# A decoder layer on one core: attention's step order, bias and clears moved, and the next phase's first rows loaded ahead of the barrier

## What is computed

```python
# x: 4 batches x 512 tokens x 512 channels
x = layernorm(x + attention(x))   # 16 heads of 32 channels, causal, softmax, output projection with bias
x = layernorm(x + chosen(x))      # one of 4 SwiGLU experts per token, chosen by the token id
x = layernorm(x + routed(x))      # top 2 of 8 SwiGLU experts (F = 352) plus a shared one (1408)
```

## Time and profile before

| | |
|---|---|
| median of 3 runs | 1285.53 us (1281.93, 1285.53, 1288.90) |
| the profiled execution | 1281.12 us |
| its span, first to last instruction | 1279.4 us |
| attention phase | from 0 to 459.4 us |
| chosen phase | 459.4 to about 599 us |
| routed phase | from there to the end |
| PE busy over the span | 1183.3 us, 92% |
| DVE, ACT, POOL busy | 691.8, 455.7, 238.2 us |

### The profile page before, as it was taken

The page is one execution under the profiler, slowest core; times in us unless marked ns, Lnnn a source line. Parts: engine busy times, 40 slices in busy tenths (PEclk is TensorE's granted clock), DMA queues, the critical chain, the costliest instruction groups (busy, mean ns, idle before and its releaser), DMA issues.

```text
span 1279.4 us, 20171 instructions
## 1 busy us (share of the span) xinstructions
PE 1183.3 (92%) x6404; PEld 938.2 (73%) x6404; DVE 691.8 (54%) x1469; ACT 455.7 (36%) x698; POOL 238.2 (19%) x358
## 2 busy tenths in 40 slices
PE   7788999999999769995999999999999999899996
PEld 5555566566576558884678888899999998678885
DVE  5664556656657546664547744444344432676754
ACT  3244334433435222221433334244444443333331
POOL 2021312412513410002300441000000000433200
PEclk8989999999999879997899999999999999999998
DMA  7355663532523322223523566344444531656440
GB/s 241 84 168 163 222 187 106 151 93 51 141 64 89 108 82 83 83 83 94 170 74 99 177 223 211 92 150 138 150 152 146 186 106 42 205 178 199 142 140 33
DMA packets 129276, 169.72 MB, mean 133 GB/s; under 512 B 17552, under 2 KB 70800, under 8 KB 129168
## 3 DMA queue, kind: packets, MB, share of 16 engines
q1 hardware_dynamic: 115360, 136.64, 34.7%
q0 software_dynamic: 8496, 28.32, 6.6%
q10 hardware_dynamic: 5312, 3.42, 1.1%
HBM read 95.98 MB, written 47.19 MB: 112 GB/s over the span
## 4 chain that ended last, share of the span: by engine, by line
PE 52%; DVE 4%; POOL 2%; issue 2%; DMA 2%; ACT 1%; SPq 0%; ACTq 0%; DVEq 0%; POOLq 0%
PE routed_ps L808 17%; PE routed_ps L1361 16%; PE chosen_psG L808 4%; PE chosen_psY L808 4%; PE routed_ps L1380 2%; PE routed_ps L1381 2%; PE routed_ps L1382 2%; POOL routed_rows_io L1299 2%; PE routed_ps L1402 1%; DVE routed_held L1704 1%; PE routed_ps L1425 1%; PE chosen_psX L889 1%; DMA routed_wdraw<-in_L_ffn_Wd_dram 1%; PE chosen_psH L908 1%; PE routed_ps L1326 1%
## 5 line engine op out<-in xcount | busy, mean ns | idle before, releaser
L459 PE MATMUL psT<-store 128*128 128x512 f32 x576 | 159.9, 412 | 5.1 <-DVE store L673 3.2
L742 DVE CUSTOM_DVE_ANT_0 psS<-psS,attn_mask 128x512 f32<-128x512 f32 (+3 forms) x256 | 120.6, 514 | 54.6 <-PE psS L525 54.5
L629 ACT ACTIVATE acc<-psE 128x512 f32<-128x512 f32 x160 | 92.9, 598 | 147.5 <-PE psE L546 143.5
L1361 PE MATMUL routed_ps<-routed_later,routed_held 128*128 128x512 f32 x528 | 124.7, 392 | 5.9 <-issue 2.9
L1361 PE MATMUL routed_ps<-routed_first,routed_held 128*128 128x512 f32 x528 | 127.6, 395 | 1.4 <-DVE routed_first L1800 1.4
L459 PEld LDWEIGHTS psT<-store 128*128 128x128 f32 x576 | 108.1, 198 | 26.0 <-issue 3.9
L1361 PEld LDWEIGHTS routed_ps<-routed_later,routed_held 128*128 128x128 f32 x528 | 98.3, 188 | 30.1 <-DVE routed_held L1704 6.6
L808 PE MATMUL routed_ps<-routed_held,routed_h_hi 128*128 x624 | 116.3, 328 | 0.6 <-DVE routed_h_lo L1745 0.6
L1361 PEld LDWEIGHTS routed_ps<-routed_first,routed_held 128*128 128x128 f32 x528 | 99.4, 190 | 22.1 <-DVE routed_first L1800 1.8
L1299 POOL DMA_INDIRECT routed_rows_io<-sorted_y,routed_pos x32 | 37.5, 1173 | 388.1 <-DMA sorted_y<-routed_rows_io 314.3
L402 POOL TENSOR_SCALAR_AFFINE_SELECT acc<-acc 128x256 f32<-128x256 f32 (+1 forms) x160 | 56.9, 361 | 282.8 <-ACT acc L629 281.9
(11 more groups left out here) (248 smaller groups left out, 1980.1 us busy)
## 6 DMA issues: line engine op xcount, KB each, us to landing
sorted_x<-attn_zero SPq DMA_DIRECT2D x19, 768.0 KB, 4.7
routed_sraw<-in_L_ffn_Sg_dram SPq DMA_DIRECT2D x44, 256.0 KB, 3.1
routed_sraw<-in_L_ffn_Su_dram SPq DMA_DIRECT2D x44, 256.0 KB, 3.6
routed_sraw<-in_L_ffn_Sd_dram SPq DMA_DIRECT2D x44, 256.0 KB, 3.9
routed_rows_io<-sorted_x SPq DMA_DIRECT2D x39, 256.0 KB, 2.9
sorted_y<-routed_rows_io SPq DMA_DIRECT2D x39, 256.0 KB, 2.2
attn_qS<-attn_ch_hi SPq DMA_DIRECT2D x128, 64.0 KB
attn_kS<-attn_ch_hi SPq DMA_DIRECT2D x112, 64.0 KB
```

The lines of the kernel that those rows point to most:

```text
L459: last = pe.matmul(out, lhs[a](k), rhs[c](k), start=(s[-1] == 0 and k == 0), stop=(s[-1] == 2 and k == KC - 1))
L629: act.activation(p_f[:, u, :], psE[:, n % 2, :], ACT.Exp, scale=SCALE).then_inc(exp_done, 1)
L742: last = dve.tensor_tensor_reduce(scores, scores, mask[:, (3 - t) * P:T], 1.0, BELOW_ALL, ALU.add, ALU.max, rowmax[:, g % 2, t, i:i + 1])
L1361: last = pe.matmul(out, w[:, slot, at + k * P:at + (k + 1) * P], x_part(k), start=(g == 0 and k == 0), stop=(g == 2 and k == KC - 1))
```

## The change

1. `LZ` and `ZB` for the last batch stand earlier, and so do `LN2` and `ST` of the batch before. `ZB` is done in four instructions, one per tile, and for the last batch they stand between the `PV` steps of iteration 15. DVE waits for each tile's own bias. A `pool.drain()` stands ahead of the last group's `PV`.
2. `XT` blocks 0 and 1 of the next batch stand behind the first two `PV` steps of the iteration; blocks 2 and 3 of batch 1 behind the first two pairs.
3. The first `P1` unit of a group stands one product later in the head; so three of them lie in the head, not four.
4. SP issues the clears four at a time, behind the key stack only.
5. The first four loads of sorted rows are issued by SP at the end of the attention phase, as soon as all scatters are out, ahead of the barrier. They go into the last four tiles of `acc`, which replace `chosen_xs`.
6. ACT runs one small Silu ahead of the first copy of the chosen phase.

```diff
-        fill = []
+        fill, early, soon = [], [], []
...
-            fill += turn[:2] + out[0] + out[1] + out[2] + turn[2:] + out[3]
+            fill += (out[0] + out[1] + out[2] + turn[2:] + out[3]) if b else []
+            early = turn[:2]
+            soon = [] if b else turn[2:]
...
-            steps += [one] + left[n:n + 1] + (p1[n - 2:n - 1] if n >= 2 else [])
+            steps += [one] + left[n:n + 1] + (p1[n - 3:n - 2] if n >= 3 else [])
...
-                steps += [("PV", s - 1, j)] + p1[n:n + 1] + p2[n:n + 1]
-                if n == 1 and at == 3 and b:
+                steps += [("PV", s - 1, j)] + p1[n:n + 1] + p2[n:n + 1] + early[n:n + 1]
+                if s == NG - 2 and n < 2:
+                    for i in (2 * n, 2 * n + 1):
+                        steps += [("LN2", b - 1, i), ("ST", b - 1, i)]
+                if s == NG - 1:
+                    steps += [("ZB", b, n)]
+                if n == 1 and at == 3 and b and b < B - 1:
                     steps += [("LZ", b)]
...
-        if at == 3:
-            steps += [("ZB", b)]
+        if at == 3 and b < B - 1:
+            steps += [("ZB", b, i) for i in range(QT)]
...
-    steps += [("PV", NG - 1, j) for j in order] + [("NH", 0), ("CW", 9), ("NH", 1)]
+    steps += [("DR",)] + [("PV", NG - 1, j) for j in order] + [("NH", 0), ("CW", 9), ("NH", 1)]
...
-                    if g >= 3:
-                        for _ in range(min(2, len(pieces))):
+                    if g >= 3 and qk == 1:
+                        for _ in range(min(4, len(pieces))):
                             clear()
...
             sp.wait_ge(x1_out, 16 * QT * B)
+            for s in range(4):
+                sp.dma_start(acc[:, NT - 4 + s, :], sorted_x1[s * P:(s + 1) * P, :]).then_inc(xs_in[s], 16)
...
-                    pool.tensor_tensor(z[:], z[:], bp[:].unsqueeze(1).broadcast_to([P, QT, C]), ALU.add).then_inc(zb_done, 1)
+                    pool.tensor_tensor(z[:, i, :], z[:, i, :], bp[:], ALU.add).then_inc(zb_done, 1)
...
-            for s in range(4):
-                load_x(s)
             for s in range(NS):
...
+            act.activation(silu[:, 1, 0:1], ident[:, 0:1], ACT.Silu)
             high_x(0)
```

More of the change, by code:

```diff
@@ L87, in attention_steps @@
         for m, one in enumerate(p2):
-            one = [one] + norm[m:m + 1]
+            one = [one] + norm[m:m + 1] + soon[m:m + 1]
             if m in (6, 9) and s == 0:
@@ L95, in attention_steps @@
             steps += [("YH", s - 1)]
-        if at == 2 and b:
+        if s == NG - 2:
+            steps += [("LZ", B - 1)]
+        elif at == 2 and b:
             for i in range(QT):
                 steps += [("LN2", b - 1, i), ("ST", b - 1, i)]
-        if at == 3:
-            steps += [("ZB", b)]
+        if at == 3 and b < B - 1:
+            steps += [("ZB", b, i) for i in range(QT)]
     b = B - 1
-    steps += [("PV", NG - 1, j) for j in order] + [("NH", 0), ("CW", 9), ("NH", 1)]
+    steps += [("DR",)] + [("PV", NG - 1, j) for j in order] + [("NH", 0), ("CW", 9), ("NH", 1)]
     steps += product("PR", b, 0) + product("PR", b, 1) + [("LN1", b, 0)]
@@ L109, in attention_steps, with attention_phase @@
     return steps
-def attention_phase(nc, sems, acc, store, ident, powm, pos, table, x, w_attn, b_attn, w_proj, b_proj, tokens, ctx_w, sorted_x1, sorted_x2):
+def attention_phase(nc, sems, acc, store, ident, powm, xs_in, pos, table, x, w_attn, b_attn, w_proj, b_proj, tokens, ctx_w, sorted_x1, sorted_x2):
     B, T, C = x.shape
@@ L408, in _ @@
                 elif kind == "ZB":
-                    b = s[1]
+                    b, i = s[1:]
                     if b == 0:
                         pool.wait_ge(bias_in, 32)
-                        for i in range(QT):
-                            pool.wait_ge(x0_in[i], 16)
-                            pool.wait_ge(sh_full[bank_of["XT", 0, i]], use_of["XT", 0, i] + 1)
+                        pool.wait_ge(x0_in[i], 16)
+                        pool.wait_ge(sh_full[bank_of["XT", 0, i]], use_of["XT", 0, i] + 1)
                     else:
                         pool.wait_ge(z_in, 16 * b)
-                    pool.tensor_tensor(z[:], z[:], bp[:].unsqueeze(1).broadcast_to([P, QT, C]), ALU.add).then_inc(zb_done, 1)
+                    pool.tensor_tensor(z[:, i, :], z[:, i, :], bp[:], ALU.add).then_inc(zb_done, 1)
                 elif kind == "LN1":
@@ L432, in _ @@
                                             in_=z[:, i, :], in_offset=None).then_inc(x1_out, 16)
+                elif kind == "DR":
+                    pool.drain()
                 elif kind == "LZ":
@@ L779, in _ @@
                     dve.wait_ge(sh_full[bank_of[s[:3]]], use_of[s[:3]] + 1)
-                    if i == 0:
-                        dve.wait_ge(zb_done, b + 1)
+                    dve.wait_ge(zb_done, b * QT + i + 1)
                     dve.tensor_tensor(z[:, i, :], psT[:, bank_of[s[:3]], :], z[:, i, :], ALU.add).then_inc(sh_free[bank_of[s[:3]]], 1)
@@ L810, in products, with chosen_phase @@
     return last
-def chosen_phase(nc, sems, store, ident, powm, table, C, sorted_x, sorted_y, E):
+def chosen_phase(nc, sems, store, ident, powm, xs_in, table, C, sorted_x, sorted_y, E, acc):
     KC = C // P
@@ L824, in chosen_phase @@
         w_hi, w_lo = chosen_weights(store, E, KC, C)
-        xs = sb("xs", [P, 4, C], F32)
+        xs = acc[:, acc.shape[1] - 4:, :]
         xT_hi = [sb(f"xT_hi{r}", [P, KC, P], F32R) for r in range(2)]
@@ L840, in chosen_phase @@
         psY = ctx.enter_context(nc.psum_tensor("chosen_psY", [P, 2, 512], F32))
-        xs_in = [sem(f"xs_in{r}") for r in range(4)]
         x_turned = sem("x_turned")
@@ L1930, in decoder_kernel @@
         x2_in = [sems.enter_context(nc.semaphore(f"x2_in{n}")) for n in range(T // P + B - 1)]
+        xs_in = [sems.enter_context(nc.semaphore(f"xs_in{n}")) for n in range(4)]
         acc = keep.enter_context(nc.sbuf_tensor("acc", [P, NT, C], F32))
@@ L1933, in decoder_kernel @@
             store = weights.enter_context(nc.sbuf_tensor("store", [P, 2 * E * KC * C], F32R))
-            attention_phase(nc, sems, acc, store, ident, powm, pos, table, x, w_attn, b_attn, w_proj, b_proj,
+            attention_phase(nc, sems, acc, store, ident, powm, xs_in, pos, table, x, w_attn, b_attn, w_proj, b_proj,
                             itok.rearrange("b s -> (b s)"), ctx_w, sx1, sx2)
-            stored = chosen_phase(nc, sems, store, ident, powm, table, C, sx1, sy1, E)
+            stored = chosen_phase(nc, sems, store, ident, powm, xs_in, table, C, sx1, sy1, E, acc)
         routed_phase(nc, sems, ident, powm, acc, x2_in, pos, sy1, stored, out.rearrange("b s d -> (b s) d"), sx2, sy2, (wr, wsg), (wg, wu, wd), (sg, su, sd))
```

2 lines of the change are left out of this document (1 added, 1 removed).

## The result

The changed kernel takes 1271.7 us in the median of 7 runs (1269.57 to 1275.86); the kernel before, run in turn with it on the same chip, 1280.3 us in 7 (1275.82 to 1288.9). The ratio is 0.9926, 95% interval 0.9903 to 0.9949; by it the changed kernel takes 9.4 us less, between 6.5 and 12.4. The profiled execution took 1269.57 us with a span of 1267.7, 11.7 less than before.

A forecast was written before the change was run, and what follows sets the result against it. PE, busy 92% of the span, was taken as the bound, so gains are its waits or low clock. Terms -5.6 - 2.4 - 2.6 + 2.0 - 3.6 - 1.8 = -14.0 us from 1281.1 gave 1267.1; stated 1269, range 1259 to 1279.

The forecast's parts named there:

- those for being right: PE's waits: `attn_yT_lo` below 3 us, `attn_x_in` at most about 1, turned blocks about 3; barrier about 12 us sooner.
- sign of being wrong: Attention: long clears with stack waits, late POOL selects, or waits for `attn_rowmax` and Q's low part summing to over 8 us.
- part 4: Attention heads: one score unit later lengthens some waits and shortens others, +2.0 us in sum; bounds -1.5 and +8.
- Part 1: Attention, batch 1 turned sooner: load and split waits and slow clock mostly go, 5.6 us gained; bounds 3 and 7.1.
- Part 2: Stacks of groups 4 and 5: clears behind the key stack, cycle 21.8 us, 2.4 us gained in sum.
- the bound without a stall: Key stack clears: if four are issued without a stall, the cycle is PE's 18.5 us and the gain 5.7 us.
- full hold-up: Rival at the clears: four hold up the next stack fully, costing 3.5 us; total 1275 us, chance 0.12.
- Part 3: Attention, batches 2 and 3 turned sooner: the projection's 1.34 us wait goes twice, 2.6 us gained; bounds 0 and 2.6.
- the rival on the slower side: Score unit's 1.1 us on DVE exposed in 14 groups: costs 19 us, total 1286; chance 0.14 with other losses.
- Part 5: End of attention: `ZB` no longer collides with `NH`; projection 2.3 us sooner, 1.3 of clock, 3.6 gained; bounds 0 and 5.9.
- POOL last: Rival at attention's end: `z` lands late, `PV` of group 15 waits 2.3 us more, no gain; 1273 us, chance 0.10.
- Part 6: Switch from attention to the chosen phase: sorted rows loaded ahead of the barrier, gain 1.9 less 0.1 us; bounds 0.5 and 2.7.

The follow-up runs named there:

- second measurement: The changed kernel itself, unaltered, timed and profiled again; ratio to the kernel before 0.9945 (0.9919 to 0.9971).
- experiments 3: Changed kernel with two clears behind each query stack and two behind each key stack again; ratio to the kernel before 0.9964 (0.9938 to 0.9990).
- 6: Changed kernel with batch 1 turned where it was before, clears staying behind the key stack; ratio to the kernel before 0.9974 (0.9953 to 0.9995).
- kernel 12: Kernel before with only the early turn of batch 1 and clears in fours behind the key stack; ratio to the kernel before 0.9939 (0.9916 to 0.9962).
- kernel 4: Changed kernel with two clears behind each key stack over ten groups, instead of four; ratio to the kernel before 0.9915 (0.9883 to 0.9947).
- kernel 1: Changed kernel with the score units in all heads back where they were; ratio to the kernel before 0.9908 (0.9877 to 0.9940).
- 2: Changed kernel with the old head in the first group alone; ratio to the kernel before 0.9935 (0.9910 to 0.9959).
- kernel 8: Changed kernel with z of batches 1 and 2 loaded and biased one iteration later; ratio to the kernel before 0.9909 (0.9879 to 0.9940).
- kernel 9: Changed kernel with old head, later z load, and clears only where the next stack has time; 1263.6 us, ratio to the kernel before 0.9826.
- experiment 7: Changed kernel with the end of attention as before, except the bias stays in four instructions; ratio to the kernel before 0.9931 (0.9910 to 0.9951).
- experiment 11: Changed kernel with the four loads of sorted rows issued behind the barrier again; ratio to the kernel before 0.9946 (0.9926 to 0.9967).

## Why the prediction was right, and where it was not

The time forecast, 1269 us, is 2.7 us from the measured 1271.7, and the direction and most mechanisms were right. The gain was forecast too large: 14 us on one profile, where 6.5 to 12.4 were measured (7 us by the ratio of the second measurement). The time came close partly by luck, since the kernel before, too, took 5 us less over 7 runs than in the 3 that were shown.

Of the signs that the prediction named, those for being right came in PE's waits: `attn_yT_lo` at 2.1 us, no row for `attn_x_in`, turned blocks at 3.2. Attention did not end 12 us sooner: DVE's last subtraction starts at 449.88 us instead of 458.47, 7.1 us sooner counted from M(0), and 0.5 in the second profile. And one sign of being wrong came: the waits for `attn_rowmax` and for the low part of Q sum to 3.9 + 10.3 = 14.2 us, where over 8 was named. It belongs to part 4. By its steps:

- **Part 1, batch 1.** Forecast -5.6, measured M(1) to M(2) -5.8 and -4.3. The waits named are gone; one of 1.87 us for a split stands at 92.07, where about 1.5 us were left to wait. What the step lacked: it gave the whole gain to the early turn, though the load of block 2 was also held by the clears of part 2 (experiments 3, 6 and 12).
- **Part 2, clears.** Forecast -2.4 for M(2) to M(5) by a cycle of 21.8 us; the changed kernel's cycle was 21.2 to 21.3 us where it was waited for, and the sum -1.5 and -1.1. SP was held by the third and fourth clear: four issues took 3.7 us, where 2.3 would have been free of stalls and SP was assumed busy for 5.3. The query pieces took 6.5 to 7.3 us, 1.5 to 2.3 more (1.4 assumed). Two clears in a row were issued in 1.14 us, and M(2) to M(5) of kernel 4, 6.5 us shorter than before, is near the 5.7 us of the bound without a stall. The loss at each of two stacks (rival "full hold-up") did not come.
- **Part 3, batches 2 and 3.** Forecast -2.6, with the old head -1.8 in each of the two iterations (30.78 us in both in kernel 1, against 32.63 and 32.56; 32.52 in kernel 12, which has the old turns), -3.6: better than forecast.
- **Part 4, the head.** This is the step that failed in its size: forecast +2.0. Measured +2.6 in the first group (experiments 1 and 2), and 4.3 us over M(5) to M(15) between kernels 8 and 9, both at full clock (these also differ in the places of the clears). `M`'s wait was put at 0.42 us. It was 0.43 at M(5), M(6), M(9), M(10) and M(13), but 1.1 to 1.4 at seven others, so pricing the lost cover by the unit's own 0.24 us was too little. Against kernel 1, which has the unit back in the head, the waits at `M` are 9.1 us more in sum, those for ACT 2.7 less (-1.2 forecast) and those for `attn_rowmax` 0.9 less (+2.1 forecast). In the first group a unit more falls among the pairs, where DVE has the work on `chosen_pos` and `chosen_table` too: its wait of 0.86 us at 68.33 is new. It stands in a stretch of low clock that is longer than before. This is not one execution's chance: over M(0) to M(1) the granted clock was 0.65 to 0.68 in seven of the eight profiles with the new head (0.76 in kernel 8) and 0.74 to 0.80 in the six with the old one. Which wait keeps it low isn't settled. The window of it in the changed kernel:

```profile
68.00:72.00 4.00, 3.67 (x11) 3.28 (x12) 3.39 (x19) 0.87 (x3) 0.86 (x2) 0.50 0.11 28
```

  PE is at half clock for all of it; before, the granted clock from 68 to 72 us was 0.64, and full from 72 us on. With some 7 us in all, part 4 is between the forecast and the rival on the slower side (19 us): the rival's price was right in kind, and what came is a third of its size.
- **Part 5, the end.** Forecast -3.6, measured -2.6 and -2.3 to the projection, and -1.6 and -3.2 behind it together with part 6. The step's times held: counted from M(15), the projection was forecast at 433.7 - 412.48 = 21.2 us and came at 21.01. `PV` waited 0.79 us for POOL, and the rival "POOL last" fell, since `z` landed in 6.0 us, at 415.00. But by experiment 7 the moves themselves give little in this stretch. The cut of the addition in four, which I had priced at nothing, bounds the collision and gave about 0.8 us there. A piece took 1.29 us and not 1.12. Much of the rest is that the collision had been near its worst before, which is chance: in kernel 12, whose end is that of before, DVE's subtraction began 2.9 us into the addition and not 0.14, took 1.86 us instead of 4.64, and M(15) to PR was 22.55 us.
- **Part 6, the switch.** Forecast -1.8, measured -1.1 to -1.5 (experiment 11). SP issued the loads 1.65 us sooner relative to DVE's last subtraction, but the first tile came 3.10 us after it (449.21 to 452.31) and not 2.74.
- **What no step had:** 2.0 and 1.3 us from X to R. The order of steps there is the same. In all profiles of this study that stretch took either 140.6 to 141.7 us or 142.9 to 143.4, with the last product of the chosen phase at half clock in the longer ones, so I count it as chance.

The slower rival asked for 1.6 us a group. It would have needed DVE's whole time for a unit to be bare; it is about 0.45 us a group behind M(5).

## What to carry to other kernels

Two edits at one resource must be priced together: the early turn alone gave 2.3 us and the moved clears 0.4, both 4.2 to 5.8, because the load that the turn waits for lay behind the clears. Large transfers without a deadline (clears, a reload of 1 MB) belong where the next small, awaited transfer has time: in short iterations four clears in a row delayed the next stack, while kernel 9, the fastest, has four in a row where long iterations follow. Take a second profile of an unaltered kernel before explaining a difference of a few us: two of this one differed by 7.5 us over the same code.

## What the hardware did that was not expected

- DVE's subtraction of two SBUF tiles does not run beside POOL's addition but ends right behind POOL's instruction in progress: 4.64 us beside one of 4.49, 1.86 us beside the rest of one of 4.51 (kernel 12: POOL from 431.80, DVE from 434.73), 1.55 us beside additions of 1.29, and 0.42 us alone.
- The same wait is followed by a lower clock in one execution and not in the next. In both profiles of the changed kernel PE waits for the split of batch 1's block, 1.87 and 1.92 us. The windows behind it, first profile and then second:

```profile
92.00:96.00 4.00, 3.93 (x20) 3.41 (x21) 1.92 (x9) 2.08 (x4) 2.02 (x3) 1.00 0.69 237
```

```profile
93.00:97.00 4.00, 3.99 (x14) 3.37 (x15) 1.85 (x9) 1.61 (x3) 1.64 (x2) 0.69 0.91 340
```

  The granted clock is 1.00 in one and 0.69 in the other, and M(1) to M(2) takes 20.82 or 22.37 us. This pair of values (20.8 to 20.9 or 22.4) comes back in all kernels with both edits. One profile thus can't price a wait's share of the clock.
